# Cross-attention kernel: each batch's last 65 context tokens projected once at the start and reloaded, three equal parts a batch, and split query weights

## The reference

```python
q = query @ Wq.T + bq
k = key_value @ Wk.T + bk
v = key_value @ Wv.T + bv
scores = einsum('bhqd,bhkd->bhqk', q, k) / sqrt(32)
attn = stablemax(scores)            # s = x + 1 where x >= 0, else 1 / (1 - x); s / sum(s)
context = einsum('bhqk,bhkd->bhqd', attn, v)
```

## Time and profile before

| | us |
|---|---|
| median of 3 runs | 1272.31 (1272.18 to 1272.36) |
| the profiled execution | 1272.52 |
| its span in the profile | 1270.8 |
| outside the span | 1.7 |
| PE busy in the span | 1260.8 (99%) |
| mean granted TensorE clock | 0.999 of full speed |

### The profile page before, as it was taken

How to read it: one execution, slowest core, us unless ns; L and a number is a source line. 1 busy time by engine, 2 the same in 40 slices (tenths; PEclk the granted TensorE clock), 3 DMA queues, 4 the chain that set the end, 5 groups by cost and what they waited for, 6 DMA issues and landing times.

```text
span 1270.8 us, 29915 instructions
## 1 busy us (share of the span) xinstructions
PE 1260.8 (99%) x13126; PEld 1097.3 (86%) x13126; DVE 649.4 (51%) x936; ACT 634.2 (50%) x1085; POOL 437.4 (34%) x203
## 2 busy tenths in 40 slices
PE   9999999999999999999999999999999999999998
PEld 8888888888788888888789789798989999999997
DVE  5333453444463363463354454766776555565655
ACT  4445454464545544545444646646544443554443
POOL 1445345544555545545546535200032000100000
PEclk9999999999999999999999999999999999999999
DMA  6131011021011012012012111764556499999990
GB/s 244 50 103 51 18 56 50 23 68 67 19 64 68 18 56 101 19 64 68 18 51 105 51 56 43 284 255 157 179 195 224 148 348 365 340 344 347 357 396 35
DMA packets 32775, 174.89 MB, mean 138 GB/s; under 512 B 5944, under 2 KB 8152, under 8 KB 14464
## 3 DMA queue, kind: packets, MB, share of 16 engines
q1 hardware_dynamic: 30896, 168.16, 36.0%
q0 software_dynamic: 1744, 4.76, 1.2%
HBM read 166.84 MB, written 6.06 MB: 136 GB/s over the span
## 4 chain that ended last, share of the span: by engine, by line
PE 98%; DVE 1%; DMA 0%; ACT 0%; issue 0%; DVEq 0%; SPq 0%
PE bank L740 23%; PE bank L728 22%; PE bank L1079 11%; PE sc L1096 9%; PE sc L756 8%; PE sc L941 7%; PE bank L769 4%; PE sc L960 3%; PE bank L960 3%; PE bank L833 1%; PE bank L796 1%; PE bank L887 1%; PE bank L898 1%; PE sc L898 1%; DMA ctxt<-in_ctx 0%; PE sc L999 0%
## 5 line engine op out<-in xcount | busy, mean ns | idle before, releaser
L587 POOL TENSOR_TENSOR xn<-xn,tt 128x1024 f32<-128x1024 f32 x96 | 230.1, 2397 | 330.9 <-DVE tt L1325 329.7
L1208 ACT ACTIVATE tt<-sc 128x512 f32<-128x512 f32 (+1 forms) x208 | 107.8, 602 | 351.5 <-PE sc L756 351.4
L1423 DVE TENSOR_TENSOR wsl<-ring,wsh 128x2048 fp32r<-128x2048 f32 x72 | 166.8, 2316 | 111.0 <-ACT wsh L1163 107.9
L1312 DVE TENSOR_SCALAR kk<-bank,bkt 128x512 f32<-128x512 f32 (+2 forms) x130 | 80.8, 622 | 213.6 <-PE bank L728 213.2
L728 PE MATMUL bank<-cxh,wkh 128*128 128x512 f32 (+2 forms) x512 | 181.1, 354 | 1.5 <-DVE va L1320 1.0
L728 PE MATMUL bank<-cxl,wkh 128*128 128x512 f32 (+2 forms) x512 | 174.6, 341 | 0.0
L728 PE MATMUL bank<-cxh,wkl 128*128 128x512 f32 (+2 forms) x512 | 174.1, 340 | 0.0
L740 PE MATMUL bank<-wvh,cxh 128*128 128x512 f32 (+1 forms) x416 | 163.5, 393 | 0.0
L740 PE MATMUL bank<-wvl,cxh 128*128 128x512 f32 (+1 forms) x416 | 162.7, 391 | 0.0
L740 PE MATMUL bank<-wvh,cxl 128*128 128x512 f32 (+1 forms) x416 | 162.2, 390 | 0.0
L1163 ACT CAST wsh<-ring 128x2048 fp32r<-128x2048 f32 x72 | 137.4, 1909 | 48.0 <-PE sc L1096 20.9
(11 more groups left out here) (270 smaller groups left out, 2024.2 us busy)
## 6 DMA issues: line engine op xcount, KB each, us to landing
ring<-in_w SPq DMA_DIRECT2D x112, 1024.0 KB, 6.1
ctxt<-in_ctx SPq DMA_DIRECT2D x15, 1024.0 KB, 4.9
ctxt<-in_ctx SPq DMA_DIRECT2D x8, 642.0 KB, 3.9
ctxt<-in_ctx SPq DMA_DIRECT2D x10, 512.0 KB, 3.6
wqt<-in_wo SPq DMA_DIRECT2D x4, 1024.0 KB, 4.8
wqt<-in_aq SPq DMA_DIRECT2D x4, 1024.0 KB, 5.3
wqt<-in_ap_ SPq DMA_DIRECT2D x4, 1024.0 KB, 6.9
yrows<-K SPq DMA_DIRECT2D x1, 2048.0 KB, 9.1
```

The lines of the kernel that those rows point to most:

```text
L587: e.tensor_tensor(dacc[0:kn, y, :], dacc[0:kn, y, :], tt[0:kn, w, :], ALU.add).then_inc(s["da_pool"], 1)
L1423: e.tensor_tensor(wsl[m % 3][:], ring[slot(unit_split(m))][:], wsh[m % 3][:].bitcast(F32), ALU.subtract).then_inc(s["wl_dve"], 1)
```

## The change

- A batch's tokens 0 to 1535 are three parts of 512; there are 24 parts, all alike. `key_groups` puts one group a slot in a batch's slots 0 to 11. Slot 12 has none.
- The 65 last tokens of all eight batches come in one load (`tails`, 520 columns: 2 x (4 x 64 + 4)). At the start `tail_keys` makes their keys (96 matmuls of 260 columns), `tail_values` their values (four groups of 128 tokens, one of the eight odd tokens: 60 matmuls of 512 columns). Both are stored to DRAM (`ktail`, `vtail`) and reloaded batch by batch by SP (`load_tail` in slot 1 of the batch, `load_tail_values` in slot 11).
- `values(n)` is no longer called for the 65-token chunk. The values of slot 10 fall away in each batch (its chunk 12); the last four full chunks are made in their own slots 99 to 102.
- `first_keys` and the 256-token halves are gone. Batch 0's first part (512) is projected after the queries.
- x transposed and Wq are split into high and low halves (ACT, DVE, POOL); the queries are 48 fp32r matmuls of 512 columns.
- Rows of `kk`, `cxh`, `cxl` and `ctxt` are 520 elements apart instead of 512 (`WID`); pads shift later buffers; the reserve for software descriptors is 4096 bytes a partition (`dynamic_dma_scratch_size`).

```diff
-SPANS = ((0, 512), (512, 512), (1024, 256), (1280, 321))
-HALVES = ((0, 256), (256, 256))
-WID = 512
+WID = 520
+TAIL = 65
-NPART = len(PARTS)
+NPART = 3 * NB
...
 def key_groups(slot):
     for i in range(1, NPART):
         f = first(i - 1)
-        if chunks_of(i - 1) == 4:
-            early += [(i, slot - f)] * (0 <= slot - f < 4)
-        elif chunks_of(i - 1) == 2:
-            early += [(i, 0)] * (slot == f) + [(i, 2)] * (slot == f + 1)
-            late += [(i, 1)] * (slot == f) + [(i, 3)] * (slot == f + 1)
-        else:
-            early += [(i, 0)] * (slot == f) + [(i, 2)] * (slot == f + 1) + [(i, 3)] * (slot == f + 2)
-            late += [(i, 1)] * (slot == f)
+        groups += [(i, slot - f)] * (0 <= slot - f < 4)
...
 def values_in(slot):
-    if slot + 2 < NCH - 3:
-        return slot + 2
-    return slot if NCH - 3 <= slot < NCH else None
+    if slot + 2 < NCH - 5:
+        return None if is_tail(slot + 2) else slot + 2
+    return slot if NCH - 5 <= slot < NCH - 1 else None
...
+            def tail_keys():
+                for c in range(4):
...
+                    for x_, (a, b) in enumerate(((0, 0), (1, 0), (0, 1))):
...
+                        for g in range(4):
+                            m = e.matmul(bank[4 + g][:, 0:260], (wkh, wkl)[a][:, c, g * P:(g + 1) * P],
+                                         (cxh, cxl)[b][:, 1, c, 0:260], start=(x_ == 0 and c == 0),
+                                         stop=(x_ == 2 and c == 3))
...
+            def tail_values(j):
+                dst, kn = take("vt", j), (8 if j == 4 else P)
+                col = 260 * (j // 2) + P * (j % 2)
+                if j < 2:
+                    e.wait_ge(s["kt_dve"], 8 + 2 * j + 2)
...
             def turn(t, dst):
                 e.wait_ge(s["xn_dve"], t + 1)
+                if t < 2:
+                    e.wait_ge(s["kt_dve"], 16)
+                else:
+                    e.wait_ge(s["xt_dve"], t - 1)
...
-            first_keys()
+            tail_keys()
...
+            tail_values(0)
+            tail_values(1)
             for t in range(2):
                 turn(t, bank[2 + t])
...
+            tail_values(2)
             for t in range(2, 4):
                 turn(t, bank[t])
...
+            tail_values(3)
+            tail_values(4)
+            e.wait_ge(s["xt_dve"], 4)
             for g in range(4):
-                queries(g, 1)
+                queries(g)
+            for g in range(4):
+                keys(0, g)
             for n in range(2):
                 values(n)
...
+                if n % PER == 1:
+                    load_tail(n // PER)
+                if n % PER == PER - 2:
+                    load_tail_values(n // PER)
...
-    nc = bacc.Bacc("TRN2", target_bir_lowering=False, num_devices=1)
+    nc = bacc.Bacc("TRN2", target_bir_lowering=False, num_devices=1, dynamic_dma_scratch_size=4096)
```

More of the change, by code:

```diff
@@ L45, in first, with is_tail, tokens, place @@
 def first(i):
[L47 to L63, removed]
+    return PER * (i // 3) + 4 * (i % 3)
+def is_tail(n):
+    return n % PER == PER - 1
+def tokens(n):
+    return TAIL if is_tail(n) else P
+def place(n):
+    b, j = divmod(n, PER)
+    return 3 * b + j // 4, j % 4
+def formed(n):
+    return (PER - 1) * (n // PER) + n % PER
 def key_groups(slot):
-    early, late = [], []
+    groups = []
     for i in range(1, NPART):
         f = first(i - 1)
-        if chunks_of(i - 1) == 4:
-            early += [(i, slot - f)] * (0 <= slot - f < 4)
-        elif chunks_of(i - 1) == 2:
-            early += [(i, 0)] * (slot == f) + [(i, 2)] * (slot == f + 1)
-            late += [(i, 1)] * (slot == f) + [(i, 3)] * (slot == f + 1)
-        else:
-            early += [(i, 0)] * (slot == f) + [(i, 2)] * (slot == f + 1) + [(i, 3)] * (slot == f + 2)
-            late += [(i, 1)] * (slot == f)
-    return early, late
+        groups += [(i, slot - f)] * (0 <= slot - f < 4)
+    return groups
 def ending(slot, lag):
@@ L161, in projections @@
 def projections():
-    uses = [("k", 0, g) for g in range(4)] + [("v", 0), ("v", 1)]
+    uses = [("vt", j) for j in range(5)] + [("k", 0, g) for g in range(4)] + [("v", 0), ("v", 1)]
     for n in range(NSLOT):
-        early, late = key_groups(n)
         for d, what in STEPS:
@@ L171, in projections @@
         uses += [("d", b) for b in finished(n)[0]]
-        uses += [("k", i, g) for i, g in early + late]
+        uses += [("k", i, g) for i, g in key_groups(n)]
         if values_in(n) is not None:
@@ L575, in sums @@
             def sums(n):
-                kn, w, y = chunk(n)[2], n % TR, (n // PER) % 2
+                kn, w, y = tokens(n), n % TR, (n // PER) % 2
                 e.wait_ge(s["f_dve"], 2 * n + 2)
@@ new lines, in tail_values @@
+            def tail_values(j):
[3 more added lines that the diff above has]
+                    e.wait_ge(s["kt_dve"], 8 + 2 * j + 2)
+                if j == 4:
+                    e.wait_ge(s["tl_dve"], 3)
+                for c in range(4):
+                    if j == 0 and c % 2 == 0:
+                        e.wait_ge(s["wvl_dve"], c // 2 + 1)
+                    for x_, (a, b) in enumerate(three):
+                        m = e.matmul(dst[0:kn, :], (ceh, cel)[a][:, c, :] if j == 4 else
+                                     (cxh, cxl)[a][:, 1, c, col:col + P], (wvh, wvl)[b][:, c, :],
+                                     start=(c == 0 and x_ == 0), stop=(c == 3 and x_ == 2))
+                m.then_inc(s["vt_pe"], 1)
@@ L1032, in pe @@
                     denominators(b)
-                for i, g in early + late:
+                for i, g in key_groups(n):
                     keys(i, g)
@@ L1201, in act @@
                 for m in group(n):
-                    kn = chunk(m)[2]
+                    kn = tokens(m)
                     if m >= TR:
@@ L1210, in act @@
                 for m in group(n):
-                    w, kn = m % TR, chunk(m)[2]
+                    w, kn = m % TR, tokens(m)
                     for hb in range(2):
@@ L1487, in vector @@
                     rows(0, t)
-            for g in range(4):
-                keys(0, g)
-            turned(3, bank[3])
-            e.wait_ge(s["wvh_act"], 1)
-            e.tensor_tensor(wvl[:], wvt[:], wvh[:].bitcast(F32), ALU.subtract).then_inc(s["wvl_dve"], 1)
+                for g in range(2 * h, 2 * h + 2):
+                    tail_keys(1, g)
+            for j in range(2):
+                tail_values(j)
+            for t in range(2):
+                turned_lo(t, bank[2 + t])
+            tail_values(2)
+            for t in range(2, 4):
+                turned_lo(t, bank[t])
+            for j in range(3, 5):
+                tail_values(j)
             e.wait_ge(s["small_in"], 224)
@@ L1502, in vector @@
             e.tensor_copy(kio[:], iotai[:, P:P + 120].rearrange("p (k e) -> p k e", e=8)).then_inc(s["iota_dve"], 1)
-            values(0)
-            values(1)
+            for g in range(4):
+                keys(0, g)
+            for n in range(2):
+                values(n)
             count = [0]
@@ L1646, in vector @@
                     weights(m, 1)
-                for i, g in early:
+                for i, g in key_groups(n):
                     keys(i, g)
@@ L1651, in vector @@
                     weights(m, 1)
-                for i, g in late:
-                    keys(i, g)
                 for b, g, m in finished(n)[1]:
```

342 lines of the change are left out of this document (211 added, 131 removed).

## The result

| | kernel before | kernel after |
|---|---|---|
| median of 4 runs, us | 1272.34 (1272.18 to 1272.54) | 1285.18 (1283.71 to 1286.25) |
| profiled execution, us (its span) | 1272.5 (1270.8) | 1285.57 (1283.8) |
| ratio | 1 | 1.0100, interval 1.0083 to 1.0118 |

The forecast was 1261.6, the range 1258.5 to 1267.5. The result lies 23.6 us above the one and 17.7 above the top of the other, on the other side of no change.

What follows compares the result with a forecast made beforehand. TensorE, busy for 99% of the span, was taken as the bound. The loop's 38.8 us saved less a start 28.0 later gave 10.8, a count check 10.4; 10.7 was taken from 1272.3, giving 1261.6, range 1258.5 to 1267.5.

Steps and rivals of the forecast that it cites:

- The start: Before the loop: tail keys, tail values and queries put the loop's first scores at 63.5 us, 28.0 later than before.
- the end of batch 7: Last batch, up to output(3): keys 2.0 and gate 0.3 saved, 0.4 lost, so 1.9 saved; stage predicted at 89.5 us.
- Slot 12's wait: Each batch's slot 12, now without keys: TensorE waits for DVE's weights of chunk 12, 1.7 us lost in all.
- The idle time near the end: Batch 7, before the last chunk's `weighted`: with the values of 103 gone, TensorE idles for about 2.3 us.
- 12 matmuls of 512 still at 2.72: Attention loop: a sign that 12 matmuls of 512 columns keep their earlier price of 2.72 us, 0.227 each.
- Part 1: The attention loop, all eight batches: fewer key and value matmuls, less new waits, 38.8 us saved.
- the expert stages keep their matmuls; buffers only move: Stages after the attention loop: no change in time; that stretch predicted at 457.7 us, as before.
- a spacing above 0.23: 512-column matmuls: a sign that would make the prediction wrong, against 0.227 us each.
- the rival: Pitch of 520 slows matmuls of L728 and L740: 2304 at 0.007, 16 us, giving 1277.6, slower; chance 0.08.
- The clock: Rival: idle of 2.3 us before the last chunk's `weighted` drops the clock to 1.2 GHz; 5 us, 1266.6; chance 0.03.
- batches 1 to 6: Middle of the loop: keys 2.0 and values 2.7 saved, 4.7 a batch, 28.2 for six before waits; predicted 563.6 us.
- the other waits in the loop: Slot 10's pair, keys in slot 13, context and tail reloads: all held covered, taken at nothing.

Runs made afterwards that it cites:

- b_pitch520: Kernel before with rows of kk, cxh, cxl and ctxt 520 elements apart instead of 512, and pads behind them: 1281.46 us, ratio 1.0071.
- a_pitch512: Kernel after with rows 512 elements apart again, pads gone, tails' buffers laid differently and the first part's high half formed later: 1274.53 us, ratio 1.0016.
- a_all: Kernel after with three edits: rows of 512, weights_split(0) behind the copy of the values, shared_up(0) in slot 103: 1266.75 us, ratio 0.9957.
- a_split_late: Kernel after with DVE's weights_split(0) one slot later, behind the copy of the values of chunk 100: 1279.11 us, ratio 1.0053.

## Why the prediction was wrong, point by point

**What held.** The start: 63.3 for 63.5, in part by luck. The first tail matmul came at 7.99 and not at 7.5, the work after it took about 0.7 longer than 54.6, and the waits of 1.2 us that the sum had did not come: TensorE's waits show none between the first tail key and the loop. Batch 0 and the end of batch 7, once the causes below are taken away: 85.8 for 85.7, and 89.6 for 89.5 (though of the wait of 2.3 us that the 89.5 hold only 0.8 is left there, so about 1.5 us of other waits had not been counted). Slot 12's wait: 1.9 us in all for 1.7. The idle time near the end: 2.2 for 2.3. The reloads: no wait of TensorE for a DMA has appeared. The descriptor reserve: nothing.

**The largest single step: the price of a matmul was carried over.** "12 matmuls of 512 still at 2.72" was an assumption in every term of Part 1, and "the expert stages keep their matmuls; buffers only move" was the whole of the last step. Both were priced at zero, and the price is 10.7 us by the medians, 9.6 by the profiled spans: forecast plus 10.7 is 1272.3, no change at all. The prediction's own sign, a spacing above 0.23, came. That the kernel is slower, and not the same, takes the end of batch 7 as well. It was among the rivals, with 0.08, at 16 us. The size was within a factor of 1.5; the chance was low, and the reason wrong. The weights' rows stay 2048 bytes apart, so not "all operands" lie 2080 apart, and it is the distance to the weights that changes. Against the rival I set the 322-column operands in buffers of a pitch of 512, which follow the line; but by the sizes of the buffers the operands of every projection of the kernel before lie a multiple of 256 bytes apart, and 322-column matmuls don't slow in `b_pitch520` either, so those rows could not speak of that. The rest of the kernel was left out of the rival as well: 3.4 of the 10.7 us are there, or 3.7 against the last column of the table.

**The step that missed 9.7 us: the end of batch 7.** Three parts. DVE's queue: I followed TensorE's order and the time of the weights, and not the copies of the values, which no longer came two slots ahead; so `weights_split(0)` in front of one of them was not seen (3.0 us). The clock: given 0.03 at 5 us for the one wait that I knew of; it fell in both waits, for about 2.4 and 2.6 us. 5 us is what both cost together; the one that I knew of cost half. The chance should have been far higher, as the earlier trace rows show a fall in the kernel before in the only stretch with so little work. The rest is the spacing (eleven groups at 0.07, 0.8 us) and three other waits of 0.4 to 0.7 us, at L949 and ahead of scores, of which the forecast had 0.4 in all.

**The step that missed 9.8 us: batches 1 to 6.** 4.9 of it is the spacing (573.4 against 568.5 in `a_pitch512`). The other 4.8 are still in `a_all`: 0.8 us a batch. A batch without a token tile takes 88.5 us, 87.6 in `a_all`, for the 86.9 of the prediction. Part of the 0.8 is in slot 4, whose values wait for DVE's copy. The chain of `a_all` in batch 1, then two lines of POOL's timeline there:

```profile
176.41 1.74 DVE xT L1568
178.17 2.29 DVE cTh L1570
...
182.33 0.24 DVE cTh L1570
...
182.80 0.70 DVE va L1428
183.49 0.04 issue
183.54 3.04 PE bank L812 x12
```

```profile
173.41 4.58 POOL L622 TENSOR_TENSOR cxl<-ctxt,cxh 128x2048 fp32r<-128x2048 f32 x1
177.95 2.42 POOL L636 TENSOR_TENSOR xn<-xn,tt 128x1024 f32<-128x1024 f32 x1
```

Operations of DVE that take 0.30 and 0.24 us at their second turn took 1.74 and 2.29 at the first. They ended at 178.14 and 180.45, 0.15 and 0.08 us after POOL's two operations (177.99 and 180.37), and it is so in all six batches; so DVE seems to wait for POOL here, though no run takes POOL's work away. The copy of the values behind them is late, TensorE waits for 0.5 us, and the group then takes 3.04 instead of 2.72. Slots 4 and 5 so take 14.9 us where their own groups add up to 14.1; in the kernel before it was 11.7 for 11.5. That is 0.6 of the 0.8, and the later batches show 0.5 to 0.65 there too. Slots 0 and 1 of batches 3 and 5 take 0.35 us more than before, with the wait of L946, and slot 12 loses 2.2 us in the six batches (4.85 to 5.18 from its scores to the next, for 4.65 without a wait) where the sum had 1.7. That leaves 0.4 us in all that was not traced. The step that failed is "the other waits in the loop": inside a batch I had looked at the weights' way and POOL's, and not at the copies of the values behind DVE's other work.

The sum of causes against the forecast, from the medians: 10.7 (place of operands), 6.1 (the order in DVE's queue) and 4.8 (the wait at the end, of which the forecast held 2.3 already) are 21.6 alone and 18.4 together. `a_all` is 5.2 above the forecast by its median and 4.3 by its profiled span, which is the 4.8 of batches 1 to 6 less some tenths elsewhere.

## What to carry to other kernels

When a change alters a buffer's row length or puts a buffer in front of others, no matmul's price may be carried over: compute for each matmul how far its two operands lie apart modulo 256 bytes before and after. Here zero kept the price and 128 did not. Where a step is moved later in one engine's queue, walk down every other queue for what now waits behind something longer, at the seams of the loop above all. And a TensorE wait of 2 to 3 us is to be priced at about twice its length, as the clock fell in both that this kernel had; the one that was filled by moving a group of matmuls gave both back.

## What the runs showed of the hardware that was not expected

- **Distance of the operands.** With fp32r operands of which one is 128x128 and the other 128x512, a distance of 128 bytes modulo 256 between their places costs 0.003 to 0.005 us a matmul (0.2285 to 0.2325, 1.8%): 7.8 us in the kernel before with a gap of 128 bytes. Rows of 520 and pads cost 9.1. At 256, 512 and 2048 bytes there is none (1272.38 to 1272.46). Matmuls of 256 and 322 columns don't show it (1.42 for 12, 3.57 for 24). Why this is so, no run here can tell.
- **DVE beside POOL.** The same subtraction of 128x2048 took 4.02 us where POOL's two sums ran from 788.45 to 793.34, and 2.33 as a mean of 72: 1.7 us more, and 1.9 us is what the two had in common. The kernel before had it too: 4.10 us in one of its 72. The Trainium skill (SBUF — State Buffer, SBUF: two separate sides) says that a DVE operation with two SBUF inputs and a GpSimd operation that reads SBUF need the same pair of ports, and that whichever starts first has it for its whole instruction while the other waits. The trace agrees: 4.02 is about 1.9 of waiting and 2.1 of work, where the operation takes 2.28 to 2.30 with POOL idle. No run here moves POOL's sums away to show it.
- **The clock after a wait.** The granted clock fell to 0.73 in the stretch with the wait of 3.04 us and to 0.85 in the one with a wait of 2.2 us of `a_split_late`, and it stayed at 1.00 in `a_all`, where no wait in that part is longer than 0.8 us.
